# Attention units of a fused kernel: sums on four column tiles, one rounding moved to ScalarE, VectorE's unit in a new order

## What is computed

```python
qn = _l2norm(qh, axis=-2)                       # 8 heads of 64 features
kn = _l2norm(kh, axis=-2)
qk = ALPHA * jnp.einsum('bhdq,bhdk->bhqk', qn, kn)
sm = jax.nn.softmax(qk, axis=-1)                # keys are summed here
out = jnp.einsum('bhqk,bhdk->bhdq', sm, vh)
...
x = x + _L0_xattn_ref(_layernorm(x, axis=-1), ctx_2048, ctx_2048)
x = x + _L0_ffn_ref(_layernorm(x, axis=-1), ...)   # router: top 2 of 4 experts, capacity 512
```

## Time and profile before

| what | value |
|---|---|
| median of 3 runs | 620.23 us |
| profiled execution: its time, its span | 620.21 us, 618.40 us |
| PE busy | 580.6 us, 94% of the span |
| DVE, ACT, POOL busy | 354.2, 281.2, 187.3 us |
| mean granted TensorE clock | 0.978 of full speed |

### The profile page before, as it was taken

How to read it: one execution, slowest core, us unless ns; L and a number is a source line. 1 busy time by engine, 2 the same in 40 slices (tenths; PEclk the granted TensorE clock), 3 DMA queues, 4 the chain that set the end, 5 groups by cost and what they waited for, 6 DMA issues and landing times.

```text
span 618.4 us, 8885 instructions
## 1 busy us (share of the span) xinstructions
PE 580.6 (94%) x2921; PEld 409.9 (66%) x2924; DVE 354.2 (57%) x701; ACT 281.2 (45%) x421; POOL 187.3 (30%) x142
## 2 busy tenths in 40 slices
PE   8999999999998636999999999999999999999994
PEld 3445555554554413788888888888888788888883
DVE  6889898998988783543344633444534355423212
ACT  3877767767777220532433434324324324333220
POOL 8465566566552216000310420400510401500002
PEclk9999999999999957999999999999999999999997
DMA  4623323423213115223323452333451532542001
GB/s 147 205 69 121 120 88 118 136 87 119 86 53 103 68 68 187 86 74 131 117 87 134 141 188 80 119 112 109 157 183 68 157 113 81 172 157 68 1 0 68
DMA packets 46600, 67.73 MB, mean 110 GB/s; under 512 B 8560, under 2 KB 25072, under 8 KB 46576
## 3 DMA queue, kind: packets, MB, share of 16 engines
q1 hardware_dynamic: 42736, 54.84, 26.8%
q0 software_dynamic: 3840, 12.59, 6.0%
HBM read 54.70 MB, written 12.64 MB: 109 GB/s over the span
## 4 chain that ended last, share of the span: by engine, by line
PE 69%; DVE 5%; issue 1%; DMA 1%; ACT 1%; POOL 0%; POOLq 0%; DVEq 0%
PE two L1456 29%; PE four L1486 9%; PE four L1485 9%; PE four L1483 9%; PE two L1292 3%; PE four L1282 2%; PE two L1304 1%; DMA x_got<-x2n_dram,idx_all 1%; DVE junk L1059 1%; PE bank_t L1320 1%; PE bank_m L1444 1%; PE four L1327 1%; PE bank_t L1444 1%; PE bank_t L1312 1%; DVE onehot L1146 0%
## 5 line engine op out<-in xcount | busy, mean ns | idle before, releaser
L772 ACT ACTIVATE h_f<-two 128x512 f32<-128x512 f32 x64 | 38.3, 599 | 229.2 <-PE two L1456 229.2
L1222 DVE TENSOR_TENSOR h_lo<-h_f,h_hi 128x512 fp32r<-128x512 f32 x64 | 44.1, 690 | 123.7 <-ACT h_hi L773 123.7
L1456 PE MATMUL two<-xt_hi,w_hi 128*128 (+1 forms) x256 | 101.9, 398 | 0.7 <-ACT xt_hi L761 0.7
L1486 PE MATMUL four<-w_hi,h_lo 128*128 128x512 f32 x256 | 100.5, 393 | 0.0
L1483 PE MATMUL four<-w_hi,h_hi 128*128 128x512 f32 x256 | 100.5, 392 | 0.0
L1485 PE MATMUL four<-w_lo,h_hi 128*128 128x512 f32 x256 | 100.4, 392 | 0.0
L1456 PE MATMUL two<-xt_hi,w_lo 128*128 (+1 forms) x256 | 100.3, 392 | 0.0
L1456 PE MATMUL two<-xt_lo,w_hi 128*128 (+1 forms) x256 | 100.1, 393 | 0.0
L666 ACT ACTIVATE prob<-four,rnorm 128x512 f32<-128x512 f32 x128 | 77.6, 690 | 28.4 <-POOL rnorm L478 19.0
L1190 DVE TENSOR_TENSOR w_lo<-raw,w_hi 128x2048 fp32r<-128x2048 f32 x31 | 71.0, 2290 | 23.3 <-ACT w_hi L699 23.3
L478 POOL TENSOR_TENSOR rnorm<-ss_max,power 128x8 f32<-128x8 f32 x32 | 64.7, 2025 | 49.7 <-DVE ss_max L821 43.8
(11 more groups left out here) (182 smaller groups left out, 758.3 us busy)
## 6 DMA issues: line engine op xcount, KB each, us to landing
raw<-in_L_ffn_W SPq DMA_DIRECT2D x64, 512.0 KB, 4.5
x_all<-in_x SPq DMA_DIRECT2D x16, 256.0 KB, 2.8
c_sb<-in_ctx SPq DMA_DIRECT2D x16, 256.0 KB, 2.9
out<-x_all SPq DMA_DIRECT2D x16, 256.0 KB, 2.0
x2n_dram<-x2n SPq DMA_DIRECT2D x16, 256.0 KB, 2.0
p_inv<-inv_dram SPq DMA_DIRECT2D x30, 128.0 KB, 2.9
few<-p_sum SPq DMA_DIRECT2D x30, 2.0 KB, 2.2
cst<-in_consts SPq DMA_DIRECT2D x1, 354.5 KB, 5.0
```

The lines of the kernel that those rows point to most:

```text
L772: nc.scalar.activation(h_f[m % 2][:, :], z_ps[m % 2][:, :], ACT.Gelu)
L1222: nc.vector.tensor_tensor(h_lo[m % 2][:, :], h_f[m % 2][:, :], h_hi[m % 2][:, :].bitcast(F32), ALU.subtract).then_inc(h_split, 1)
L1456: return nc.tensor.matmul(z[:, :], w_part[c][:, w], x_k, start=start, stop=stop)
L1486: last = nc.tensor.matmul(acc_ps[:, t, :], h_lo[m % 2][:, h], w_hi[c][:, w], start=False, stop=(m == MT - 1))
```

## The change

The sums go onto four column tiles of 32, one for each half sum, and are no longer added in PSUM except in the last unit; so `few` has two parts for each head, which SP brings with four transfers where it had two, and DVE adds them (`few_sum`) before the reciprocal. `q_hi` is a copy of `q_f` by ACT, placed ahead of the exponentials of tile 2. DVE's unit begins with `q_f` of u+1; then come the layer norm of u+2, the first instruction of the statistics of u+3, `x2n` of u-3 (before: of u-2, at the end of the unit), the rest of the statistics, and `q_lo`. The logits of u-3 end the unit. GpSimd writes `k_lo` of u+1 at the start of the unit, once the layer norm of u+2 is written (before: of u+2, at the end). SP's order and TensorE's order are not changed. The hardware loop covers units 6 to 11.

```diff
@@ run_units
-            with engine.Fori(2, last - 1) as h:
-                unit((h, 0), 4, 3)
-                unit((h, 1), 4, 3)
...
+            unit((2, 0), 4, 3)
+            unit((2, 1), 5, 3)
+            with engine.Fori(3, last - 1) as h:
+                unit((h, 0), 5, 3)
+                unit((h, 1), 5, 3)
...
@@ spread_inverse (SP)
-                    sp.dma_start(few[half, :], p_sum[DH * h:DH * h + 1, :]).then_inc(few_in, 16)
+                    for m in range(2):
+                        row = QUAD * (2 * m + h)
+                        sp.dma_start(few[half, m * FEW:(m + 1) * FEW], p_sum[row:row + 1, :]).then_inc(few_in, 16)
@@ unit (POOL)
+                if ahead and behind:
+                    pool.wait_ge(xn_done, n + 3 if ahead > 1 else UNITS)
+                    key_remainders(after(u))
                 if ahead:
                     if behind:
                         pool.wait_ge(exp_done, TT * n)
                     key_norms(after(u))
...
-                if ahead > 1:
-                    if behind > 1:
-                        pool.wait_ge(x2n_done, n - 1)
-                    key_remainders(after(after(u)))
@@ ACT
+            def round_queries(u):
+                act.wait_ge(q_done, number(u) + 1)
+                nc.scalar.activation(q_hi[u[1]][:, :], q_f[:, :], ACT.Copy).then_inc(qhi_done, 1)
...
                     take_v(after(u), behind + 1)
+                if ahead:
+                    round_queries(after(u))
                 exponentials(u, 2, behind > 0)
@@ queries (DVE)
-                nc.vector.scalar_tensor_tensor(q_hi[u[1]][:, :], x_norm[u[1]][:, :], ALPHA, bank_m[:, :],
-                                               ALU.mult, ALU.mult).then_inc(qhi_done, 1)
+
+            def query_remainders(u):
+                n = number(u)
                 dve.wait_ge(q_done, n + 1)
                 dve.wait_ge(qhi_done, n + 1)
-                if follow is not None:
-                    normalize(follow)
                 nc.vector.tensor_tensor(q_lo[u[1]][:, :], q_f[:, :], q_hi[u[1]][:, :].bitcast(F32), ALU.subtract
@@ invert_few (DVE)
-                dve.wait_ge(few_in, 32 * (n + 1))
-                nc.vector.reciprocal(few_inv[:, :], few[:, :]).then_inc(few_done, 1)
+                dve.wait_ge(few_in, 64 * (n + 1))
+                nc.vector.tensor_tensor(few_sum[:, :], few[:, 0:FEW], few[:, FEW:2 * FEW], ALU.add
+                                        ).then_inc(few_added, 1)
+                dve.wait_ge(few_added, n + 1)
+                nc.vector.reciprocal(few_inv[:, :], few_sum[:, :]).then_inc(few_done, 1)
@@ unit (DVE)
+                if ahead:
+                    queries(after(u))
+                if ahead > 1:
+                    normalize(after(after(u)))
                 if ahead > 2:
                     statistics(after(after(after(u))))
+                if behind > 2:
+                    normalize_x2(before(before(before(u))), behind > 4)
+                if ahead > 2:
+                    gather_statistics(after(after(after(u))))
...
                 if ahead:
-                    queries(after(u), after(after(u)) if ahead > 1 else None)
+                    query_remainders(after(u))
                     sum_key_squares(after(u))
...
                 if behind > 2:
                     take_logits(before(before(before(u))))
-                if behind > 1 and ahead:
-                    normalize_x2(before(before(u)), behind > 3)
@@ sums (PE)
-                        last = nc.tensor.matmul(o_ps[1][DH * h:DH * (h + 1), :], cst[:, C_ONES:C_ONES + DH],
-                                                half_sum[h][n][:, :], start=(n == 0), stop=(n == 1))
+                        if ahead:
+                            row = QUAD * (2 * n + h)
+                            last = nc.tensor.matmul(o_ps[1][row:row + QUAD, :], cst[:, C_ONES:C_ONES + QUAD],
+                                                    half_sum[h][n][:, :], start=True, stop=True,
+                                                    tile_position=(0, row))
...
@@ unit (PE)
-                    pe.wait_ge(qhi_done, n + 2)
+                    pe.wait_ge(q_done, n + 2)
                     transpose_queries(after(after(u)))
```

More of the change, by code:

```diff
@@ L39 @@
 FEW = 2 * D // P
+QUAD = P // 4
 DVE_HEADS, POOL_HEADS = (0, 1), ()
@@ L190, in xattn_moe_kernel @@
             half_sum = [[att(f"half_sum{h}{n}", [P, D]) for n in range(2)] for h in range(2)]
-            few = att("few", [P, FEW])
+            few = att("few", [P, 2 * FEW])
+            few_sum = att("few_sum", [P, FEW])
             few_inv = att("few_inv", [P, FEW])
@@ L274, in xattn_moe_kernel @@
         few_in = sem("few_in")
+        few_added = sem("few_added")
         few_done = sem("few_done")
@@ L351, in run_units @@
             unit((1, 1), 3, 3)
-            with engine.Fori(2, last - 1) as h:
-                unit((h, 0), 4, 3)
-                unit((h, 1), 4, 3)
[L355 to L358, removed]
+            unit((2, 0), 4, 3)
[3 more added lines that the diff above has]
+                unit((h, 1), 5, 3)
+            unit((last - 1, 0), 5, 3)
+            unit((last - 1, 1), 5, 2)
+            unit((last, 0), 5, 1)
+            unit((last, 1), 5, 0)
         def run_experts(engine, expert):
@@ L505, in key_remainders @@
                 pool.wait_ge(k_split, n + 1)
[L507 to L513, removed]
             def residual(u):
@@ L563, in unit @@
                     key_norms(after(u))
-                for h in POOL_HEADS:
-                    if ahead > 1:
-                        pool.wait_ge(xsq_done, n + 3)
-                    half_sums(u, 1, h, behind > 0)
                 if ahead > 1:
@@ L684, in take_sums @@
                 if reused:
-                    act.wait_ge(few_in, 32 * n)
+                    act.wait_ge(few_in, 64 * n)
                 nc.scalar.activation(p_sum[:, :], o_ps[1][:, :], ACT.Copy).then_inc(sum_taken, 1)
@@ L707, in _ @@
             round_keys((0, 1), False)
+            round_queries((0, 0))
             act.wait_ge(rk_done, 1)
@@ L790, in statistics, with gather_statistics @@
                                    ).then_inc(bn_done, 1)
+            def gather_statistics(u):
+                n = number(u)
                 dve.wait_ge(bn_done, n + 1)
@@ L829, in take_logits, with queries @@
                                         bank[:, 0:E], bgb[:, :], ALU.add).then_inc(logit_done, 1)
-            def queries(u, follow):
+            def queries(u):
                 n = number(u)
@@ L909, in _ @@
             statistics((0, 0))
+            gather_statistics((0, 0))
             normalize((0, 0))
             statistics((0, 1))
+            gather_statistics((0, 1))
             sum_query_squares((0, 0))
@@ L916, in _ @@
             sum_query_squares((0, 1))
-            queries((0, 0), None)
+            queries((0, 0))
+            query_remainders((0, 0))
             widen_queries((0, 1))
@@ L927, in _ @@
             statistics((1, 0))
+            gather_statistics((1, 0))
             done = [0]
@@ L990, in unit @@
                 if ahead:
-                    queries(after(u), after(after(u)) if ahead > 1 else None)
+                    query_remainders(after(u))
                     sum_key_squares(after(u))
-                for h in DVE_HEADS:
+                for h in range(2):
                     half_sums(u, 0, h, behind > 0)
@@ L1303, in sums @@
                     for h in range(2):
-                        last = nc.tensor.matmul(o_ps[1][DH * h:DH * (h + 1), :], cst[:, C_ONES:C_ONES + DH],
-                                                half_sum[h][n][:, :], start=(n == 0), stop=(n == 1))
+                        if ahead:
[3 more added lines that the diff above has]
+                                                    tile_position=(0, row))
+                        else:
+                            last = nc.tensor.matmul(o_ps[1][DH * h:DH * (h + 1), :], cst[:, C_ONES:C_ONES + DH],
+                                                    half_sum[h][n][:, :], start=(n == 0), stop=(n == 1))
                 last.then_inc(sums_ready, 1)
```

## The result

The changed kernel takes 664.22 us (median of 6 runs) against 620.03 us for the kernel before (6 runs): a ratio of 1.0705 with a 95% interval of 1.0664 to 1.0746. It is slower by about 44 us. One run of 755 us, whose granted clock (0.735) was far lower than that of the others, is left out of the ratio; without it the median is 662.98 us. The profiled execution took 668.2 us, with a span of 666.1 us, 47.7 us more than before; it lies above the other four (661.7 to 665.5), which has to be kept in mind where its rows are added up.

The account below looks back on a forecast made before the run. DVE was taken to set the 11.87 us period, PE closely next. Nine units at 3.88 us more give 34.9, plus 6 and 1 for the edge units: 41.9 on 620.21, so 662 us, range 642 to 678.

Parts of the forecast that it names:

- its likeliest case: DVE stands at `few`, queued on SP behind the store of `x2n`, some 3 us a unit; chance 0.62.
- not on the path: On SP's queue, the load of `c` waits for `k_lo`, which ends before SP gets there: no cost.
- Once around the loop: Attention unit, from the end of `x2n` to the next: 15.75 us against 11.87, so 3.88 more a unit.
- The block of `x2n` by `k_lo`: On DVE, `x2n` waits until POOL's `k_lo` ends: 0.78 us a unit, other end 0.
- Units 0 to 2 and 12 to 15: Edges of the attention phase: +1 us (-2.8 to +4) for units 0 to 2, +6 (3 to 9) for 12 to 14.
- The sums: PE's sums on four tiles take 0.95 us instead of 1.89, with nothing on the path.
- `q_hi`: Moved to ACT: DVE saves 0.77 us, ACT gets about 0.65; cost nothing, or some tenths if `few` came early.
- The bare way from logits to `q_f`: Between DVE's logits and `q_f`, 0.14 us to PE's values and 1.13 more lie bare: 1.27 us a unit.
- The lower clock: Rival: PE idles around its sums, its clock falls, values and spread slow: 10 us more, 672 us; chance 0.20.
- The case without a wait at `few`, 621 us: Rival: SP reaches `few` about 3 us sooner than summed, leaving DVE's loop of 11.96 us; chance 0.08.
- The PE-bound case, 607 us: Rival: `few` lands before DVE needs it, a unit is PE's own work, 10.77 us, saving 13; chance 0.07.

Follow-up runs that it names:

- the run with `few` first: Changed kernel with SP issuing the store of `x2n` and the load of `c` behind the `few` transfers instead of ahead: 624.20 us, ratio 1.0060.
- the run with the logits earlier: On top of the run with `few` first, DVE's logits ahead of the residual and widened norms ahead of the second statistics: 609.21 us, ratio 0.9831.
- the run with PE kept busy: Changed kernel with 13 more unused matmuls of 512 columns a unit around the sums, units 3 to 13: 662.44 us, ratio 1.0655.
- the last two runs: The run with the logits earlier, 609.21 us; then that plus `x2n` ahead of statistics, `k_lo` behind `x2n`, key squares ahead of `q_lo`, 609.33 us.

## Why the prediction was right, point by point

*The forecast, 662 us, and its likeliest case.* The measured 664.22 lies inside 642 to 678, and the mechanism is the one named: the run with `few` first takes 40 of the 44 us away by SP's order alone, with every other part of the change in place. The prediction named the store of `x2n`; that the load of `c`, by its wait for `k_lo`, still holds `few` about half as long once the store is out of the way, it set aside as "not on the path". That was right for the changed kernel, where the store comes first, but it hid nearly half of what the order costs.

*Once around the loop.* Forecast 15.75 us, measured 15.63. DVE stood at `few` for 2.4 to 3.2 us in units 3 to 11 (forecast some 3). That the sum came out within 0.12 us is in part luck. Over the nine units, from `q_f` to the end of `x2n` it took 2.75 us (taken: 3.00), and from the first issue of `few` to `few_sum` 3.71 (taken: 3.90, of it 2.2 for landing, which was 2.0 in the median); from PE's values to `q_f` it took 1.54 (taken: 1.13), because of the lower clock, which the sum left out. The other terms were off by 0.04 us or less. The four issues lasted 2.41 to 2.43 us in eight of the nine units (taken: 2.26) and 3.25 in one, the unit shown above.

*The block of `x2n` by `k_lo`.* Taken as 0.78 us, with 0 as the other end; `x2n` measured 1.13 to 1.22 in place of 0.53 to 0.55, about 0.6, and the run without it lost 0.64 a unit. The mechanism holds, the size was 0.15 too high: `x2n` did not begin with the end of `k_lo`, as the prediction has it, but 0.8 us ahead of it, and what was left of it after that end was shorter than a whole `x2n`.

*Units 0 to 2 and 12 to 15.* Taken as +1 and +6; measured 2.8 and 9.2, the one inside its range, the other just above it (9). This is the step that missed most, though the rows are those of an execution 4 to 5 us longer than the median, and a part of the miss may be its own. At the start DVE stood 1.73 and 2.94 us at `few` in units 1 and 2, where I had only allowed for some loss against the shorter sums. At the end units 14 and 15 too stood at `few`, 1.00 and 0.57 us, and in the stretch from 235 to 243 us the clock was 0.60; there the last unit's sums took 3.68 us, against 1.94 before. The forecast was made for one unit of the loop; its edges were estimated and not followed.

*The sums.* Forecast: half the time, and nothing gained. They took 1.06 us (0.95 estimated), PE waited for what it saved, and alone this part costs 3 us, because it brings two more transfers and an addition into DVE's way.

*`q_hi`.* Forecast: no cost, and a gain only inside DVE's own time. Alone it gives 1.3 us.

*The bare way from logits to `q_f`.* Forecast 1.27 us; the run with the logits earlier took out 1.29.

*The rivals.* The lower clock came (0.87 over the phase), but its price was mis-sized: 10 us in the prediction, 3.8 by the rows of the run with PE kept busy. Only values and spread at the head of a unit are on the path, and they were slow in five of the nine units, by 0.5 to 0.9 us (DVE's wait was up to 2.14 us there, 1.2 to 1.3 in the others). The case without a wait at `few`, 621 us, is nearly the run with `few` first, 624.20; its period is 12.36 against the 11.96 of that case, and `x2n` is held by `k_lo` there too (1.12 us). The PE-bound case, 607 us, is nearly the last two runs, 609: it needed `few` first and the logits earlier, which the change lacked.

## What to carry to other kernels

A step that is moved within one engine moves in every queue that waits for it: ask which transfers stand behind its consumer in an in-order queue, and whether the engine itself waits for one of them further on. Here a store and a load that nobody needed soon, each waiting for an instruction that the change had moved into the same unit, stood ahead of four small transfers that DVE needed at once, and turning them round was worth 40 us. The first of two such holds hides the second. And when an engine's unit ends with what another engine waits for and begins with what that one sends back, the way between them lies bare; put other work in the middle before counting what a shorter matmul may bring.

## What the runs showed of the hardware that was not expected

Four small transfers in a row on SP's queue, each one row of 512 values to 64 partitions, were issued in 2.41 to 2.43 us in eight of the units 3 to 11 and in 3.25 in the ninth of the same execution; single issues lasted up to 1.43 us against a median of 0.60. The cause stays open.

The granted clock fell in units 3 to 11, where it had been 1.00 before the change. What PE did there: in most units it stood idle for 0.6 to 2.1 us before the sums, had 1.06 or 1.07 us of work and was idle again for 1.8 to 2.0 us; the phase's mean clock was 0.87. Products that nobody uses, put into those gaps, brought it back to 0.98 over the phase, and to 1.00 from 100 us on.
